# Five of a batch's eight heads scored in halves instead of four, in a fused attention kernel

## The reference

```python
q = rmsnorm(x @ Wq.T); k = rmsnorm(x @ Wk.T); v = x @ Wv.T      # 32 query heads, 8 key heads, D = 128
q, k = rope(q, pos), rope(k, pos)
k_all = concat([k_cache[block_table], k]); v_all = concat([v_cache[block_table], v])   # 512 + 32 keys
scores = einsum(q, k_all) * SCALE;  scores = where(valid, scores, -1e30)
probs = softmax(scores);  o = einsum(probs, v_all);  return o @ Wo.T
```

## Time and profile before

| | before |
|---|---|
| median of the runs | 2344.66 us |
| the profiled execution | 2344.58 us, its span 2342.8 us |
| TensorE matmul busy | 2256.9 us, 96% |
| VectorE busy | 1705.4 us, 73% |
| ScalarE busy | 1296.5 us, 55% |
| GpSimd busy | 1145.8 us, 49% |
| attention stage, first to last mask | 746.0 to 1965.0 us of the span |

### The profile page before, as it was taken

How to read it: one execution, slowest core, us unless ns; L and a number is a source line. 1 busy time by engine, 2 the same in 40 slices (tenths; PEclk the granted TensorE clock), 3 DMA queues, 4 the chain that set the end, 5 groups by cost and what they waited for, 6 DMA issues and landing times. The chain is left out here.

```text
span 2342.8 us, 52248 instructions
## 1 busy us (share of the span) xinstructions
PE 2256.9 (96%) x16384; PEld 1951.4 (83%) x16384; DVE 1705.4 (73%) x3503; ACT 1296.5 (55%) x2643; POOL 1145.8 (49%) x1218
## 2 busy tenths in 40 slices
PE   6998999999995999999999999999999997999999
PEld 6877777777773999999999999999999996888887
DVE  7861788888884888888888888888888886422222
ACT  5832888888873555555555555555555554311111
POOL 4200454444443777777777777777777773000000
PEclk9999999999997999999999999999999998999999
DMA  6533244434436888888888888888888885643442
GB/s 257 211 108 92 86 130 128 128 122 116 127 112 219 276 298 286 298 288 292 292 290 286 283 282 290 288 293 291 288 294 291 287 293 178 204 140 94 133 131 63
DMA packets 451814, 501.70 MB, mean 214 GB/s; under 512 B 95861, under 2 KB 390773, under 8 KB 443414
## 3 DMA queue, kind: packets, MB, share of 16 engines
q1 hardware_dynamic: 414870, 366.44, 49.4%
q0 software_dynamic: 36864, 134.23, 16.3%
HBM read 408.21 MB, written 92.34 MB: 214 GB/s over the span
## 5 line engine op out<-in xcount | busy, mean ns | idle before, releaser
L1120 POOL TENSOR_TENSOR att_probs<-att_probs,att_inverse 128x512 f32<-128x512 f32 x512 | 535.1, 1045 | 287.6 <-DVE att_inverse L1316 283.1
L1224 ACT ACTIVATE att_probs<-att_probs,att_low 128x544 f32<-128x544 f32 x512 | 383.7, 749 | 515.5 <-DVE att_low L1303 515.4
L1181 PE MATMUL att_o<-att_probs_t,att_values 128*128 128x128 f32 x4096 | 540.9, 275 | 0.0
L1303 DVE CUSTOM_DVE_ANT_0 att_probs<-att_score,att_mask,att_batch_cols 128x544 f32<-128x544 f32 x512 | 400.0, 781 | 137.2 <-PE att_score L1146 99.3
L1181 PEld LDWEIGHTS att_o<-att_probs_t,att_values 128*128 128x128 f32 x4096 | 497.6, 192 | 0.0
L1312 DVE COPY att_probs_t<-att_turn 128x512 f32<-128x512 f32 x512 | 351.1, 686 | 1.2 <-PE att_turn L1161 1.2
L1106 POOL DMA_INDIRECT att_values<-L_cond_v_cache,att_v_rows_of x256 | 283.7, 1108 | 82.6 <-POOL att_v_rows_of L1102 50.1
L1146 PE MATMUL att_score<-att_keys_raw,att_queries_raw 128*128 128x288 f32 (+1 forms) x1024 | 290.6, 407 | 26.2 <-DMA att_queries_raw<-q_t 24.0
L1161 PE MATMUL att_turn<-ident,att_probs 128*128 128x128 f32 x2048 | 311.1, 274 | 1.2 <-POOL att_probs L1120 0.8
L958 POOL TENSOR_TENSOR proj_q_out<-proj_by_cos,proj_by_sin 128x512 f32<-128x512 f32 x128 | 188.2, 1470 | 217.0 <-DVE proj_by_sin L886 217.0
L1279 DVE TENSOR_TENSOR att_keys_lo<-att_keys_raw,att_keys_hi 128x384 fp32r<-128x384 f32 (+1 forms) x320 | 260.9, 816 | 16.7 <-ACT att_keys_hi L1217 16.7
(11 more groups left out here) (129 smaller groups left out, 3807.9 us busy)
## 6 DMA issues: line engine op xcount, KB each, us to landing
att_keys_raw<-L_cond_k_cache SPq DMA_DIRECT2D x1024, 128.0 KB
q_t<-proj_q_out SPq DMA_DIRECT2D x32, 1024.0 KB, 5.3
att_queries_raw<-q_t SPq DMA_DIRECT2D x64, 512.0 KB
o_t<-att_heads_out SPq DMA_DIRECT2D x64, 512.0 KB, 6.6
out_o_raw<-o_t SPq DMA_DIRECT2D x32, 1024.0 KB, 5.7
maps_even<-L_cond_weight SPq DMA_DIRECT2D x8, 1024.0 KB, 13.0
maps_odd<-L_cond_weight SPq DMA_DIRECT2D x8, 1024.0 KB, 17.0
w_nat<-L_cond_Wq SPq DMA_DIRECT2D x8, 1024.0 KB, 6.7
```

What stands on the lines that cost most here:

```text
L1120: nc.gpsimd.tensor_tensor(probs[:, k, 0:L], probs[:, k, 0:L], inverse[:, k:k + 1].to_broadcast([P, L]), ALU.mult).then_inc(probs_ready, 1)
L1181: last = nc.tensor.matmul(o, values[j][:, t, h * D:(h + 1) * D], probs_t[m % 2][:, t * P:(t + 1) * P], start=(t == 0), stop=False, skip_gr ...
L1224: nc.scalar.activation(probs[:, k, :], probs[:, k, :], ACT.Exp, bias=low[k][:, 0:1], scale=-1.0, accum_out=total[k][:, 0:1]).then_inc(exp_ ...
L1303: nc.vector.tensor_tensor_reduce(out=probs[:, k, :], in0=score_ps[:, LEFT:LEFT + KEYS], in1=mask[j][:], scale=batch_cols[j][:, h:h + 1], s ...
```

## The change

NATIVE goes from 4 to 3: head 3 of each batch is scored in halves too, and every piece of the split covers five heads instead of four (480 or 640 elements a partition instead of 384 or 512; the four buffers of the halves grow alike). ACT_FROM goes from 4 to 3 and DVE_FROM from 5 to 4: ScalarE's pieces stand at heads 3, 4, 5, 6, 7 and 0, VectorE's at 4, 5, 6, 7, 0 and 1, the mask columns at head 3. Before the first pass ScalarE makes five pieces and VectorE four, where it was four and three. SyncE's release of the key loads follows NATIVE, so it comes after head 3 instead of head 4.

```diff
--- before.py
+++ after.py
@@ -971,8 +971,8 @@
     GH = 4
     RING = 8
     PAIRS = B // 2
-    NATIVE = 4
-    ACT_FROM, DVE_FROM = 4, 5
+    NATIVE = 3
+    ACT_FROM, DVE_FROM = 3, 4
     SPLIT = HK - NATIVE
     PARTS = [slice(0, 3), slice(3, 6), slice(6, 9), slice(9, 13), slice(13, NPP + 1)]
     NP = len(PARTS)
```

## The result

The changed kernel takes 2337.79 us (median of 11 runs, 2333.55 to 2340.17), the kernel before 2343.63 in the same comparison (11 runs, 2340.95 to 2345.08): ratio 0.9976, 95% interval 0.9968 to 0.9984, so 5.8 us faster. Forecast were 2353 and a slower kernel. The direction is that of rival A, the size half of it.

What follows compares the result with a forecast made beforehand. TensorE's chain was taken to be paced by GpSimd's gathers and products and, at the loop head, VectorE's mask. Loop heads 2.8, mid-body 5.4 and ends +0.3 made +8.5 us: 2353, range 2347 to 2360, with rivals 2335 to just over 2374.

Steps and rivals of the forecast that it cites:

- rival A: GpSimd keeps its head start, gather 0 not stretched by the TENSOR_SCALAR: -10.1 us, 2335; chance 0.25.
- (1): Head 3 of 64 batches, native to split: 0.15 us cheaper each (0.10 to 0.20), -9.6 us if TensorE alone paced.
- (2): ScalarE's copies and VectorE's subtractions grow from 4 to 5 heads; on VectorE +0.10 for three, +0.13 for three.
- (3): Pieces start a head earlier; GpSimd's chain starts 0.21 earlier, gather 0 at 2.33; the moves cost nothing.
- (4): Mask's TENSOR_SCALAR inside gather 0 stretches it 0.27; subtractions stretch gathers 1 to 3 by 0.23; product 4 ends at 7.49.
- e0: Stretch of gather 0 by the mask's TENSOR_SCALAR lying inside it: taken as 0.27, between 0 and 0.34.
- the overlap rule: A gather that starts beside VectorE's work is stretched by the overlap less about 0.15; 0.34 for gather 0.
- (5): TensorE waits for product 4 at head 4's transposes, swallowing head 3's saving: +0.12 mid-body, +0.09 loop head; eviction +0.05 mid-body.
- (6): Ends: longer pieces before the first batch, +0.4 us (0 to 0.7); last batch without splitting beside it, -0.15.
- B: VectorE's piece slips in between product 3 and the group product: +0.34 a batch, 21 us, 2374; chance 0.15.
- C: TENSOR_SCALAR waits for gather 0's end; head 3's reciprocal and head 4's mask about 0.6 late: 2367; chance 0.05.
- D: The edit has no effect on the path, TensorE and VectorE both as now: 2345; chance 0.07.

Runs made afterwards that it cites:

- e2: Kernel before with only the new format: five heads split, pieces of 480 and 640, started at the old heads; ratio to before 1.0103.
- e11: Kernel before with the loop's gathers left out, values of batches 0 and 1 serving all batches; ratio to before 0.9986.
- e12: Changed kernel with the loop's gathers left out, values of batches 0 and 1 serving all batches; ratio to the kernel before 0.9947.
- e6: Changed kernel with GpSimd's four gathers spread to heads 3, 5, 7 and the next batch's head 0; ratio to the kernel before 1.0120.
- e4: Changed kernel with the mask columns put ahead of the copy of the transposes at head 3; one run, 2355.83 us.
- e1: Kernel before with only the earlier schedule (ACT_FROM 3, DVE_FROM 4), four heads split as before; 2347.38 us, ratio to before 1.0020.
- e8: Changed kernel with two spare reciprocals ahead of the mask's TENSOR_SCALAR, so it starts later in gather 0; 2356.86 us, ratio to the kernel before 1.0065.
- e3: Changed kernel with ScalarE's eviction of the outputs put ahead of its key piece at heads 2 and 6; ratio to the kernel before 0.9971.
- e10: Changed kernel with the eviction first and the gathers before the products of heads 3, 5, 6 and 7; ratio to the kernel before 0.9967.
- e13: Changed kernel with the eviction first and the gathers at heads 3, 5 and twice 6; ratio to the kernel before 1.0158.
- e9: Kernel before with the four gathers spread to heads 3, 5, 7 and head 0 of the batch needing them; ratio to before 1.0701.

## Why the prediction was wrong, point by point

(1) Head 3: right. 2.11 against 2.27, so 0.16 for the 0.15 taken.

(2) and (3) The lengths and the earlier schedule: right. Gather 0 starts at c = 2.36 for 2.33, and nothing waits for key loads in the loop. What e2 adds is that the two parts of the edit can't be had singly.

(4) Meeting GpSimd: this is the step that failed, in one term. e0 was taken at 0.27, from the neighbourhood of the 0.34 that the overlap rule gives; it is 0. Product 4 ends at c = 7.23 (1816.84 + 1.05), which is the prediction's 7.22 + e0 with e0 = 0, and product 6 ends at 12.13 (1821.74 + 1.05), its 12.13 + e0. The other terms held: gathers 1 to 3 at 1.22 to 1.23 for 1.23. The argument for a high e0 was the gather of 1.77, and that was the error of judgement: that gather had VectorE over its start as well (from 725.63, 0.29 before it, VectorE works without a pause: a TENSOR_SCALAR of 0.68, a cast, and small ones), and all the other rows had the overlap at the start too. They fitted "0 if a gather is vulnerable only in its first moments" just as well. The wait that the forecast named is real, before and after: head 4's transposes start 0.05 to 0.06 behind the end of product 4 in every steady batch of both kernels (1817.95 against 1817.89), and head 6 takes 2.80 and 2.82, against 2.69 in e11, e12 and e6, where product 4 is out of the way. (So the 0.89 from S(6) to those transposes, which the prediction took for TensorE's own, held a part of that wait: it is 0.83 to 0.84 in those kernels.) But with e0 = 0 product 4 ends at c = 7.23 instead of 7.40, GpSimd is as much earlier as TensorE is, and the 0.16 of head 3 gets through: S(7) comes at 9.20, for rival A's 9.18. With e0 = 0.27 it would have been held back until 9.45.

The section Who interferes with whom of the Trainium skill's SBUF — State Buffer says of VectorE's 2-port modes, which a TENSOR_SCALAR can be in, "Whoever issues first gets the shared pair for the whole instruction". Where VectorE's instruction is first, the trace agrees: the gather ends 0.85 to 0.88 after that instruction does, with 0.26 of it over the start (1.14, e4), 0.35 (1.20, before) or 0.64 (1.50, a subtraction in e6, at 1315.74). Where the gather is first, it does not: a TENSOR_SCALAR from 0.14 to 0.39 into it takes its ordinary length and so does the gather (e2, e6, after), and one at 0.50 to 0.55 takes 0.67 to 0.72, about 0.20 more than its ordinary 0.48, which is less than the rest of the gather (e1, e8). Subtractions taken up 0.41 to 0.74 into the later gathers of e6 are not held at all (0.81 to 0.82 for 640 elements). And the same section's inference that a tensor_tensor leaves descriptor generation alone does not hold for these gathers: gather 1 takes 1.23 with 0.36 of a subtraction over its start and 0.98 in e2 with none. A gather also reads its row numbers from SBUF; no run separates that from the writing of its descriptors.

(5) TensorE after that: the waits on VectorE were right, ScalarE's eviction was mis-sized too. It starts 0.73 after S(7) (1820.59 against 1819.86), where it was 0.42 after the earlier trace rows: 0.21 for the piece of 640 instead of 384 (0.72 against 0.51, at 1238.98), 0.16 for the earlier S(7), less 0.07 for the earlier mask. The eviction is done at 1821.16, the product that needs it starts 0.06 later and takes 1.16 for 1.06. Head 7 costs 2.35 instead of 2.20 in both halves of the body; the prediction had 0.05, in the middle only. The slip is of method: the 0.30 of slack was measured against the forecast's late S(7), and when rival A moved S(7) forward, the same slack was not worked out again. That is why A's own sum, -10.1, is twice what came.

The mask of head 0 starts at 12.81 mid-body (1823.47), A's value to the hundredth, and would let S(1) come at 13.66; but S(0) is at 11.55, and the 2.25 of head 0 makes it 13.80. At the loop head a term was missing that works the other way: S(1) no longer waits for the mask, so its group of four score matmuls takes 1.10, not 1.18, and head 1 2.38 instead of 2.46: -0.08 there. e3 shows it reversed, where S(1) waits again and head 1 takes 2.46.

(6) Ends: +0.79 in the first pass for +0.4 (0 to 0.7); the bound was just passed.

In sum, A with the eviction: 31 x (-0.11 - 0.08) + 32 x -0.01 + 0.8 = -5.4. Of the other rivals, B did not occur (the group product follows product 3 at once, 1815.03), nor C (0.48). D's 2345 is nearer to the time than the forecast, but not its mechanism: 64 x 0.16 were saved and half of it given back.

The chances were also set wrongly: A had 0.25 and the forecast 0.48 with one single row, a poor one, to separate them, and the sum tipped at e0 = 0.13. A sign that hangs on one unmeasured term inside its own bounds deserved nearer even chances.

## What to carry to other kernels

When an engine's overlap is priced by a rule read from rows, ask in which part of the instruction all those rows have it; where the new overlap lies elsewhere the rule says nothing, and both answers need about equal weight. Each rival moves the whole timeline, so every slack that the forecast used must be worked out again in the rival's own times; here an eviction with 0.30 us of slack took half the gain. And a kernel whose engines are this tightly fitted rewards no single repair: each of the wins of e3, e6 and e10 at one head was handed back at the next, or to the DMA.

## What the runs showed of the hardware

- A gather (DMA_INDIRECT on GpSimd) beside VectorE's TENSOR_SCALAR or subtraction: if that began first, the gather ends 0.85 to 0.88 after it, so 0.26 of it over the start makes the gather 1.14 (e4) and 0.36 makes it 1.23 (after), where it is 0.98 to 1.00 alone. A TENSOR_SCALAR that begins 0.14 to 0.39 into the gather costs neither anything (e2, e6, after); one at 0.50 to 0.55 loses 0.20 itself and the gather stays at 1.00 (e1, e8).
- A mask due 0.08 to 0.12 into the second of two adjoining gathers starts at least 0.75 late in 38 of 39 cases (e13); why is open.
- On TensorE, a group of matmuls whose start waited on another engine is itself about 0.1 longer (1.16 against 1.06 for eight products, 61 times in after; 1.18 against 1.08 for four native score matmuls, 90 times in before), and so is its head: such a short wait costs its own length and 0.1 more. In e12 61 groups of products take 1.15 with no gap before them, so the 0.1 also comes without a wait that the rows show.
- Gathered values whose last gather was issued three heads (6 to 7 us) ahead of their use came too late in more than half of the batches, with the DMA engines 0.86 busy (36 listed waits, up to 3.4 us, in e6) and 0.79 busy (61, up to 2.9, in e9).
